# Three order tables and one product in halves: the cross-attention part of a decoder layer on one TensorE

## The reference, cut to what matters

```python
x = x + attn(layernorm(x), ...)    # sequences in 16 heads, 64 slots: q, k with rope
    s = clip(hs @ Ws1.T @ Ws2.T + bs2); z = cumlogsumexp(s, axis=tokens); es, enz = exp(s), exp(-z)
    A = where(tril, (q @ k.T) * scale, 0)
    qv = softmax(enz * (A @ es))
    o = where(tril, (qv * enz) @ es.T, 0) @ v
    o_g = rms_norm(o) * silu(g);  return o_g @ Wo.T
x = x + xattn(layernorm(x), ctx, pos)    # 32 heads of 8 channels
    q = x @ Wq; k, v = split(ctx @ Wkv, 2, axis=-1)     # ctx: 128 tokens of 128, Wkv: 128 x 512
    q, k = axial_rope(q), axial_rope(k)
    return softmax(q @ k.T * scale) @ v @ Wout + bout
x = x + ffn(layernorm(x), ...)    # 8 experts of 128, the best two by sigmoid scores, and a shared one
    out = (silu(xt @ sw1.T) * (xt @ sw3.T)) @ sw2.T + sum over chosen experts of the same with w1, w2, w3
return x
```

## Time and profile before

| | |
|---|---|
| median of 3 runs | 602.49 us (601.88 to 605.55) |
| span of the profiled execution | 601.8 us |
| lowest run, for comparison with the span | 601.88 us |
| PE busy | 575.6 us (96% of the span) |
| DVE, ACT, POOL busy | 485.0, 371.2, 281.9 us (81%, 62%, 47%) |
| weight loads (PEld, beside PE) | 486.0 us (81%) |

### The profile page before, as it was taken

How to read it: one execution, slowest core, us unless ns; L and a number is a source line. 1 busy time by engine, 2 the same in 40 slices (tenths; PEclk the granted TensorE clock), 3 DMA queues, 4 the chain that set the end, 5 groups by cost and what they waited for, 6 DMA issues and landing times. The chain is left out here.

```text
span 601.8 us, 14128 instructions
## 1 busy us (share of the span) xinstructions
PE 575.6 (96%) x4426; PEld 486.0 (81%) x4426; DVE 485.0 (81%) x1150; ACT 371.2 (62%) x1168; POOL 281.9 (47%) x324
## 2 busy tenths in 40 slices
PE   5989999999999999999999999998789999999997
PEld 5868888888888888888888788886568878877786
DVE  6999978977977986987987798677587887887766
ACT  3438557657657567556655576676867567567453
POOL 3367754845764663764575566355762211210000
PEclk9999999999999999999999999999999999999999
DMA  8200201100200200200200000232000000000000
GB/s 277 71 0 5 85 0 36 54 2 10 78 0 0 87 0 0 87 0 0 83 4 0 19 3 1 89 92 103 3 3 11 3 11 11 3 11 11 4 10 17
DMA packets 10096, 19.34 MB, mean 32 GB/s; under 512 B 2112, under 2 KB 5696, under 8 KB 9920
## 3 DMA queue, kind: packets, MB, share of 16 engines
q1 hardware_dynamic: 10048, 18.73, 9.2%
HBM read 17.55 MB, written 1.05 MB: 31 GB/s over the span
## 5 line engine op out<-in xcount | busy, mean ns | idle before, releaser
L884 ACT ACTIVATE sa_v<-bank 128x256 f32<-128x256 f32 x64 | 24.5, 382 | 60.8 <-PE bank L268 60.8
L857 ACT ACTIVATE sa_ex<-sa_okb,sa_minus_top 128x64 f32<-128x64 f32 x128 | 42.9, 340 | 28.7 <-DVE sa_minus_top L750 26.7
L947 POOL TENSOR_TENSOR sa_qt<-sa_rope_cos,sa_rope_sin 128x512 f32<-128x512 f32 x32 | 41.1, 1286 | 39.1 <-DVE sa_rope_sin L798 38.1
L266 PE MATMUL bank<-ht_hi,sa_qk_hi 128*128 128x512 f32 x128 | 55.2, 432 | 1.3 <-DVE sa_gate L803 0.9
L947 POOL TENSOR_TENSOR sa_kt<-sa_rope_cos,sa_rope_sin 128x512 f32<-128x512 f32 x32 | 41.2, 1286 | 26.6 <-DVE sa_rope_sin L798 26.6
L266 PE MATMUL bank<-sa_vg_hi,ht_hi 128*128 128x512 f32 x128 | 53.0, 414 | 0.5 <-DVE sa_rope_sin L798 0.5
L268 PE MATMUL bank<-sa_vg_hi,ht_lo 128*128 128x512 f32 x128 | 50.5, 395 | 0.0
L267 PE MATMUL bank<-sa_vg_lo,ht_hi 128*128 128x512 f32 x128 | 50.5, 395 | 0.0
L268 PE MATMUL bank<-ht_hi,sa_qk_lo 128*128 128x512 f32 x128 | 50.5, 394 | 0.0
L796 DVE TENSOR_TENSOR sa_rope_cos<-bank,con 128x512 f32<-128x512 f32 x64 | 43.9, 686 | 7.9 <-PE bank L268 6.8
L267 PE MATMUL bank<-ht_lo,sa_qk_hi 128*128 128x512 f32 x128 | 50.2, 392 | 0.0
(11 more groups left out here) (207 smaller groups left out, 1830.1 us busy)
## 6 DMA issues: line engine op xcount, KB each, us to landing
sa_qk_raw<-in_wqk SPq DMA_DIRECT2D x8, 512.0 KB, 3.8
sa_vg_raw<-in_wvg SPq DMA_DIRECT2D x8, 512.0 KB, 3.3
sa_wo_raw<-in_wo SPq DMA_DIRECT2D x8, 256.0 KB, 2.6
xf_w_raw<-in_w SPq DMA_DIRECT2D x2, 640.0 KB, 9.0
xf_w_raw<-in_w SPq DMA_DIRECT2D x1, 1152.0 KB, 7.4
xs<-in_x SPq DMA_DIRECT2D x2, 512.0 KB, 4.7
hn<-in_w SPq DMA_DIRECT2D x2, 512.0 KB, 4.6
out<-xs SPq DMA_DIRECT2D x8, 128.0 KB, 1.7
```

Of the source, the lines that this page charges most:

```text
L266: pe.matmul(out, w_hi, m_hi, start=first, stop=False)
L857: ins = act.activation(ex[:, s, u, :], okb[:, s, u, :], ACT.Exp, bias=minus_top[:, s, u:u + 1], accum_out=total[:, buffer_of(i, g, 4), u:u ...
L947: pool.tensor_tensor(dst[:, h, c * HALF:(c + 1) * HALF], rope_cos[:, s, :], rope_sin[:, s, :], ALU.add).then_inc(roped, 1)
```

## The change

The context's product G 0 is made as two matmuls of 256 columns into the two halves of the same bank, in place of one of 512. All other edits set steps of the tables in another order; no step is added or left out, and no other instruction changes. SP's tables and POOL's table of the end stay as they are. In the opening, on PE: 6A 0 goes ahead of 6QK 0, 6A 2 ahead of 6E 1, 6VG 0 ahead of 7E 1, 6SN 1 ahead of 6A 3, 7A 2 and 6T 3 ahead of 7W 1, 7O 1 ahead of 7A 3, G 3 of sequence 2 ahead of AT; on DVE the same steps of A and QK, and 7N2 3 goes from the end of the table to a place behind S3; on ACT 6VGHI and 6WOHI go to the front, 6O 1 and 6VG 0 go ahead of others, 7WOHI ahead of 7OT 0; on POOL 6WO ahead of 6VGLO. In the steady turn, on PE: AT ahead of G 3; on DVE: DV 1 ahead of L1 6, GT and Y ahead of R 1; on ACT: U 1 ahead of T 0, HI 1 behind G 4, TT ahead of G 3, GT ahead of G 6; on POOL: S3 ahead of BIAS. In the end, on PE: L2 of sequence 7 ahead of Y 1.

```diff
@@ -1038,92 +1038,93 @@
...
 X_PE = [("L2", 0), ("G", 0), ("T", 0), ("U", 1), ("L2", 1), ("AV", 0), ("Y", 0), ("L1", 0), ("G", 1), ("U", 2),
-    ("T", 1), ("G", 2), ("AB", 0), ("AV", 1), ("L1", 1), ("Y", 1), ("AB", 1), ("T", 2), ("U", 3), ("G", 3), ("AT", 0),
+    ("T", 1), ("G", 2), ("AB", 0), ("AV", 1), ("L1", 1), ("Y", 1), ("AB", 1), ("T", 2), ("U", 3), ("AT", 0), ("G", 3),
...
-X_PE_START = [("6QK", 0, 6), ("6A", 0, 6), ("6QK", 1, 6), ("6E", 0, 6), ("6A", 1, 6), ("6ST", 0, 6), ("6QK", 2, 6),
-    ("6E", 1, 6), ("6A", 2, 6), ("6T", 0, 6), ("6SN", 0, 6), ("6W", 0, 6), ("6ST", 1, 6), ("6QK", 3, 6),
+X_PE_START = [("6A", 0, 6), ("6QK", 0, 6), ("6QK", 1, 6), ("6E", 0, 6), ("6A", 1, 6), ("6ST", 0, 6), ("6QK", 2, 6),
+    ("6A", 2, 6), ("6E", 1, 6), ("6T", 0, 6), ("6SN", 0, 6), ("6W", 0, 6), ("6ST", 1, 6), ("6QK", 3, 6),
...
-    ("7A", 1, 7), ("7E", 0, 7), ("6O", 1, 6), ("6OT", 0, 6), ("7E", 1, 7), ("6VG", 0, 6), ("6A", 3, 6), ("6SN", 1, 6),
...
-    ("6OT", 2, 6), ("6VG", 3, 6), ("7W", 1, 7), ("7A", 2, 7), ("6T", 3, 6), ("6Y", 2, 6), ("6W", 3, 6), ("7OT", 0, 7),
-    ("6VG", 4, 6), ("7E", 2, 7), ("7A", 3, 7), ("7O", 1, 7), ("7Y", 0, 7), ("G", 0, 0), ("7E", 3, 7), ("6O", 3, 6),
...
-    ("AB", 0, 0), ("AV", 1, 0), ("L1", 1, 1), ("AB", 1, 0), ("AT", 0, 0), ("G", 3, 2), ("OUT", 0, 0), ("TT", 0, 1),
...
+    ("7A", 1, 7), ("7E", 0, 7), ("6O", 1, 6), ("6OT", 0, 6), ("6VG", 0, 6), ("7E", 1, 7), ("6SN", 1, 6), ("6A", 3, 6),
...
+    ("6CS", 1, 6), ("6OT", 2, 6), ("6VG", 3, 6), ("7A", 2, 7), ("6T", 3, 6), ("7W", 1, 7), ("6Y", 2, 6), ("6W", 3, 6),
+    ("7OT", 0, 7), ("6VG", 4, 6), ("7E", 2, 7), ("7O", 1, 7), ("7A", 3, 7), ("7Y", 0, 7), ("G", 0, 0), ("7E", 3, 7),
...
+    ("L1", 0, 1), ("AB", 0, 0), ("AV", 1, 0), ("L1", 1, 1), ("AB", 1, 0), ("G", 3, 2), ("AT", 0, 0), ("OUT", 0, 0),
...
-    ("TT", 0, 7), ("OUT", 0, 6), ("T", 2, 5), ("U", 4, 5), ("Y", 1, 5), ("L2", 0, 7), ("HT", 0, 6), ("Y", 2, 5),
...
+    ("TT", 0, 7), ("OUT", 0, 6), ("T", 2, 5), ("U", 4, 5), ("L2", 0, 7), ("Y", 1, 5), ("HT", 0, 6), ("Y", 2, 5),
...
 X_DVE = [("G", 0), ("H", 0), ("T", 0), ("U", 1), ("L1", 0), ("L1", 1), ("L1", 2), ("L1", 3), ("T", 1), ("U", 2),
-    ("DV", 0), ("G", 2), ("L1", 4), ("L1", 5), ("L1", 6), ("DV", 1), ("L1", 7), ("T", 2), ("U", 3), ("OUT", 0),
-    ("S3", 0), ("T", 3), ("HN", 0), ("U", 4), ("HT", 0), ("T", 4), ("R", 0), ("R", 1), ("GT", 0), ("Y", 0), ("R", 2)]
-X_DVE_START = [("6QK", 0, 6), ("6A", 0, 6), ("6QK", 1, 6), ("6E", 0, 6), ("6A", 1, 6), ("6ST", 0, 6), ("6QK", 2, 6),
+    ("DV", 0), ("G", 2), ("L1", 4), ("L1", 5), ("DV", 1), ("L1", 6), ("L1", 7), ("T", 2), ("U", 3), ("OUT", 0),
+    ("S3", 0), ("T", 3), ("HN", 0), ("U", 4), ("HT", 0), ("T", 4), ("R", 0), ("GT", 0), ("Y", 0), ("R", 1), ("R", 2)]
+X_DVE_START = [("6A", 0, 6), ("6QK", 0, 6), ("6QK", 1, 6), ("6E", 0, 6), ("6A", 1, 6), ("6ST", 0, 6), ("6QK", 2, 6),
...
-    ("7E", 2, 7), ("7OT", 0, 7), ("FREE", 0, 0), ("7A", 3, 7), ("7Y", 0, 7), ("6VG", 4, 6), ("7N2", 0, 7),
...
-    ("S3", 0, 0), ("HN", 0, 0), ("HT", 0, 0), ("R", 0, 0), ("R", 1, 0), ("GT", 0, 0), ("R", 2, 0), ("7N2", 3, 7)]
...
+    ("7OT", 0, 7), ("7E", 2, 7), ("FREE", 0, 0), ("7A", 3, 7), ("7Y", 0, 7), ("7N2", 0, 7), ("6VG", 4, 6),
...
+    ("OUT", 0, 0), ("S3", 0, 0), ("7N2", 3, 7), ("HN", 0, 0), ("HT", 0, 0), ("R", 0, 0), ("R", 1, 0), ("GT", 0, 0),
...
-X_ACT = [("L2", 0), ("L2", 1), ("V", 0), ("L2", 2), ("L2", 3), ("T", 0), ("U", 1), ("L2", 4), ("L2", 5), ("L2", 6),
-    ("L2", 7), ("G", 1), ("AC", 0), ("T", 1), ("U", 2), ("AC", 1), ("HI", 0), ("HI", 1), ("T", 2), ("U", 3),
-    ("AT", 0), ("G", 3), ("TT", 0), ("T", 3), ("G", 4), ("U", 4), ("HT", 0), ("G", 5), ("T", 4), ("G", 6), ("GT", 0)]
-X_ACT_START = [("6W2P", 0, 6), ("6VGHI", 0, 6), ("6E", 0, 6), ("6T", 0, 6), ("6E", 1, 6), ("6SN", 0, 6), ("6T", 1, 6),
-    ("6O", 0, 6), ("6WOHI", 0, 6), ("6E", 2, 6), ("6CS", 0, 6), ("6OT", 0, 6), ("7E", 0, 7), ("6ST", 0, 6),
...
-    ("6T", 3, 6), ("6CS", 1, 6), ("6ST", 1, 6), ("7OT", 0, 7), ("7WOHI", 0, 7), ("FREE", 0, 0), ("6VG", 4, 6),
...
+X_ACT = [("L2", 0), ("L2", 1), ("V", 0), ("L2", 2), ("L2", 3), ("U", 1), ("T", 0), ("L2", 4), ("L2", 5), ("L2", 6),
+    ("L2", 7), ("G", 1), ("AC", 0), ("T", 1), ("U", 2), ("AC", 1), ("HI", 0), ("T", 2), ("U", 3), ("AT", 0),
+    ("TT", 0), ("G", 3), ("G", 4), ("HI", 1), ("T", 3), ("U", 4), ("HT", 0), ("G", 5), ("T", 4), ("GT", 0), ("G", 6)]
+X_ACT_START = [("6VGHI", 0, 6), ("6WOHI", 0, 6), ("6W2P", 0, 6), ("6E", 0, 6), ("6T", 0, 6), ("6E", 1, 6),
+    ("6SN", 0, 6), ("6T", 1, 6), ("6O", 0, 6), ("6E", 2, 6), ("6CS", 0, 6), ("6OT", 0, 6), ("6ST", 0, 6),
+    ("7E", 0, 7), ("6O", 1, 6), ("6VG", 0, 6), ("6T", 2, 6), ("6VG", 1, 6), ("7T", 0, 7), ("7E", 1, 7), ("6SN", 1, 6),
...
+    ("6VG", 3, 6), ("6T", 3, 6), ("6CS", 1, 6), ("6ST", 1, 6), ("7WOHI", 0, 7), ("7OT", 0, 7), ("FREE", 0, 0),
...
-X_POOL = [("ROT", 0), ("ROT", 1), ("LO", 0), ("LO", 1), ("BIAS", 0), ("S3", 0)]
-X_POOL_START = [("6VGLO", 0, 6), ("6WO", 0, 6), ("6QK", 0, 6), ("6E", 0, 6), ("6QK", 1, 6), ("6QK", 2, 6),
...
+X_POOL = [("ROT", 0), ("ROT", 1), ("LO", 0), ("LO", 1), ("S3", 0), ("BIAS", 0)]
+X_POOL_START = [("6WO", 0, 6), ("6VGLO", 0, 6), ("6QK", 0, 6), ("6E", 0, 6), ("6QK", 1, 6), ("6QK", 2, 6),
...
@@ -1365,7 +1366,9 @@
                         if b == 0:
                             pe.wait_ge(par_in, 16)
                             pe.wait_ge(ctx_in, 16)
-                        mm = pe.matmul(ps[:, :], ctx_all[:, b, :], wkv[:, :], start=True, stop=True)
+                        for part in range(2):
+                            half = slice(part * DIM, (part + 1) * DIM)
+                            mm = pe.matmul(ps[:, half], ctx_all[:, b, :], wkv[:, half], start=True, stop=True)
                     elif n == GT_H:
```

More of the change, by code:

```diff
@@ L1085 @@
-X_DVE_END = [("U", 1, 5), ("T", 0, 5), ("U", 2, 5), ("L1", 0, 7), ("L1", 1, 7), ("L1", 2, 7), ("DV", 0, 6),
[3 rows of a table removed]
[7 rows of a table added]
+X_DVE_END = [("U", 1, 5), ("T", 0, 5), ("U", 2, 5), ("L1", 0, 7), ("L1", 1, 7), ("L1", 2, 7), ("L1", 3, 7),
[3 rows of a table added]
     ("U", 2, 6), ("OUT", 0, 7), ("S3", 0, 7), ("Y", 0, 5), ("T", 1, 6), ("U", 3, 6), ("HN", 0, 7), ("T", 2, 6),
[2 rows of a table removed]
[2 rows of a table added]
     ("T", 3, 7), ("T", 4, 7), ("Y", 0, 7)]
-X_ACT = [("L2", 0), ("L2", 1), ("V", 0), ("L2", 2), ("L2", 3), ("T", 0), ("U", 1), ("L2", 4), ("L2", 5), ("L2", 6),
-    ("L2", 7), ("G", 1), ("AC", 0), ("T", 1), ("U", 2), ("AC", 1), ("HI", 0), ("HI", 1), ("T", 2), ("U", 3),
-    ("AT", 0), ("G", 3), ("TT", 0), ("T", 3), ("G", 4), ("U", 4), ("HT", 0), ("G", 5), ("T", 4), ("G", 6), ("GT", 0)]
@@ L1103 @@
     ("6OT", 3, 6), ("G", 3, 0), ("G", 4, 0), ("G", 5, 0), ("G", 6, 0), ("7O", 3, 7), ("V", 0, 1), ("7OT", 2, 7),
     ("G", 1, 1), ("HI", 0, 1), ("HI", 1, 1), ("7OT", 3, 7), ("G", 3, 1), ("TT", 0, 0), ("G", 4, 1), ("G", 5, 1),
[4 rows of a table removed]
-X_ACT_END = [("L2", 0, 6), ("L2", 1, 6), ("L2", 2, 6), ("U", 1, 5), ("L2", 3, 6), ("U", 2, 5), ("T", 0, 5),
[6 rows of a table removed]
-X_POOL = [("ROT", 0), ("ROT", 1), ("LO", 0), ("LO", 1), ("BIAS", 0), ("S3", 0)]
-X_POOL_START = [("6VGLO", 0, 6), ("6WO", 0, 6), ("6QK", 0, 6), ("6E", 0, 6), ("6QK", 1, 6), ("6QK", 2, 6),
[6 rows of a table removed]
-    ("ROT", 1, 1), ("BIAS", 0, 0), ("LO", 1, 1), ("7N2", 2, 7), ("WL", 0, 0), ("BIAS", 0, 1), ("ROT", 0, 2),
-    ("BIAS", 0, 2), ("WL", 1, 1), ("ROT", 1, 2), ("LO", 0, 2), ("WL", 2, 2), ("WL", 3, 3), ("S3", 0, 0), ("LO", 1, 2),
-    ("WL", 4, 4), ("7N2", 3, 7), ("WL", 5, 5), ("WL", 6, 6), ("WL", 7, 7), ("WL", 8, 8)]
[4 rows of a table added]
@@ L1127 @@
+X_ACT_END = [("L2", 0, 6), ("L2", 1, 6), ("U", 1, 5), ("L2", 2, 6), ("L2", 3, 6), ("U", 2, 5), ("T", 0, 5),
[6 rows of a table added]
+X_POOL = [("ROT", 0), ("ROT", 1), ("LO", 0), ("LO", 1), ("S3", 0), ("BIAS", 0)]
+X_POOL_START = [("6WO", 0, 6), ("6VGLO", 0, 6), ("6QK", 0, 6), ("6E", 0, 6), ("6QK", 1, 6), ("6QK", 2, 6),
[9 rows of a table added]
 X_POOL_END = [("S3", 0, 6), ("S3", 0, 7)]
```

## The result

The changed kernel takes 609.24 us (median of 4 runs, 608.29 to 611.24), the kernel before in the same runs 603.34: a ratio of 1.0095, 95% interval 1.0063 to 1.0128, or 5.7 us slower by the ratio. The forecast was 601.0, with 603.7 as its upper end. The profiled run is the one of 611.24 us, the slowest of the four; its span is 609.4, so 1.8 us lie outside the span. The forecast had taken its profiled span of 601.8 for a run of about 601.9; by this difference it was one of about 603.6.

What follows compares the result with a forecast made beforehand. PE bounds the kernel, busy 575.6 us of a 601.8 us span. Terms -0.25 - 0.66 - 0.3 + 0 - 0.3 + 0 = -1.5 from 602.49 gave 601.0 us; range 597.5 to 603.7.

Steps and rivals of the forecast that it cites:

- the opening's tail: Opening's end: 7N2 3 moved behind S3 on DVE, by_sin up to 1.1 us earlier, hn up to 0.4 later; -0.3 us.
- The steady turn: Reordered steps in each of five turns: 0 us a turn, between -0.2 and +0.5.
- The 0.2 won by GT ahead of R 1: Each turn: hid comes earlier for PE's T 0, some 0.2 us, taken back by the wait for by_sin before L2.
- The third rival: Each turn: U 1 ahead of T 0 on ACT makes L1 wait, from 0.3 us a turn; 603.5 us, chance 0.12.
- The opening's first two terms: Opening: PE's mask wait before 6A 0 goes, -0.25 us; the wait at 7Y 0 is covered, -0.66 us.
- The split product: Context's product G 0 in halves: added weight loads lie beside streaming, 0 us; 3.0 us if all exposed.
- the reading of the query's product: Same-sized float32 product in the trace before: four instructions in 0.87 us, so halves add no time.
- the rule on weight loads: Halves of G 0: loads overlap matmuls only in different row groups, so 3.0 us exposed; 604.0 us, chance 0.04.
- The end: Last sequences: L2 of sequence 7 fills PE's wait for hid_lo in front of Y 1; -0.3 us.
- The clock rival: Opening's tail: the 2.40 us gap shrinks and the 3.30 us half-clock stretch does not return; 598.8 us, chance 0.18.

## Why the prediction was wrong

**The step that failed** is the opening's tail. The prediction says that POOL's power for N2 "isn't moved and stays where it was". It was moved, from behind WL 4 to the end; and even unmoved it would have lost its wait, because DVE's variance came earlier. The prediction priced 7N2 3 on PE's and DVE's queue only. What stood on POOL's queue behind the waiting step, four subtractions of two instructions each, was held back by that wait through the router, and nobody had counted this as a gain of the kernel before. The term was -0.3, with bounds of -0.62 and +0.4; the pair alone costs 4.4 us. By the marks, 1.1 of it is hn later, where the forecast had up to 0.4 (about 0.6 of the 1.1 is hn's own length, 1.43 in place of 0.81), and some 2 the router's pieces (PE's wait for T 0 is 2.26 in place of 0.29). The rest, an estimate of 1.3, is not told apart; the lower clock on what follows is one part of it where the half-clock stretch is long.

**The mechanism** is in the rows: beside POOL's subtractions, DVE's elementwise pieces whose tiles all lie in SBUF end only when POOL's instruction has ended. In the thirteen profiles the four router pieces take 0.21 to 0.23 us in every sequence where POOL is idle, and 0.46 to 1.30 in the five openings where the subtractions run. A small tile is no protection: xf_two_plus, 128x8, takes 0.37 in place of 0.17. The reciprocal (0.20), the reduction to xf_rank (0.21) and whatever reads PSUM keep their length. The sign was on record: hn takes 0.81 in the earlier trace rows, beside POOL, and 0.41 in the steady turns of the same kernel. The Trainium skill ("SBUF — State Buffer", section "Who interferes with whom") says that a DVE instruction with two inputs in SBUF contends with a GpSimd instruction that reads SBUF, and that DVE in a 2-port mode, which `tensor_scalar` can enter, does so too. The traces agree for both: 1.30 in place of 0.22 for xf_same, 0.81 and 1.43 in place of 0.41 for hn. They don't show which port it is, nor in which mode hn runs.

**The steady turn** was taken at 0 and costs 0.28 us a turn. The 0.2 won by GT ahead of R 1 and its return at by_sin came as argued. S3 ahead of BIAS was listed among the edits that "lie on engines that are idle", at no cost. It was the same oversight: POOL's idle share says nothing of what its work does to a DVE instruction beside it. G 5 to HT went from 0.44 to 0.77 us. Against this the turn's other edits win 0.14, as the turn of 22.14 with BIAS out of the way shows; which of them does is not shown. The third rival, U 1 ahead of T 0 delaying L1, did not come: L1 starts 5.04 us behind the product, before 5.05, with no wait.

**The opening's first two terms** had the right sign and were too small: -0.4 by 381 us (forecast -0.25) and a further -0.9 by 386 (forecast -0.66), by the starts of the same PE instructions in the kernel before and in the version with 7N2 3 put back, from the common zero. PE's wait for the mask did go, and a wait of 0.84 for QK's drain took its place, as argued of DVE.

**The split product** at 0 was right, and with it the reading of the query's product; the rule on weight loads that the prediction sets against it, which would have given 3.0 us, is not borne out here. **The end**, -0.3 forecast, is -0.2 by the marks, and that is luck: the wait that was to be won stands elsewhere and stayed.

**The clock rival** had its sign the wrong way round: the gaps in the tail grew (for hn from 2.40 to 3.71, for T 0 from 0.29 to 2.26), and so did, in the profiled run, the half-clock stretch there, from 3.4 to 13.7 us.

## What to carry to other kernels

A wait is also a guard: before a step is moved so that its engine no longer waits, list what is queued behind it on that engine, and what those instructions will then run beside. VectorE and GpSimd behaved here as one resource where both work elementwise on SBUF; in a hand-written order put GpSimd's long elementwise work beside DVE's PSUM drains, and keep it away from small SBUF pieces on the critical path. Two entries moved back and one placed better turned a change of 1.0095 into one of 0.9981; a table of marks per stage found both.

## What the runs showed that was not expected

The kernel before had a granted clock between 0.988 and 1.00 from run to run and spans from 600.1 to 603.9 us on one chip, with no change of code. The stretch at 0.50 near 421 us is in five of the thirteen profiles: in one of six with the old opening's order (both moves of 7N2 3 alone) and in four of seven with the new, though the order up to that point is the same within each group. It follows PE gaps of 1.1 to 1.3 us and 0.3 to 0.6 us that all of them have. So one profile of a kernel carries 2 us or more of the clock's luck, as much as the opening's edits win, and a table of marks has to be read beside the granted clock.
